# Context keys in a strand of their own, even groups' heads copied in place, normalising on ScalarE

## The reference, cut to what matters

```python
x = _layernorm(x + gated_linear_recurrence(x))
x = _layernorm(x + window_attention(x, ctx, ctx))        # WINDOW: 4 windows of 128
x = _layernorm(x + quantised_lora_ffn(x))                # 256 -> 1024 -> 256, GELU
x = _layernorm(x + alibi_attention(x, x, x))             # ALIBI
x = _layernorm(x + masked_attention(x, ctx, ctx, group)) # MASKED: probs * group
x = _layernorm(x + latent_attention_and_moe(x))          # CAUSAL, then top 2 of 8 experts
# attention: softmax(q @ k.T / 4 (+ bias, + mask)) @ v, heads joined, @ w_out
```

## Time and profile before

| | us |
|---|---|
| median of 3 runs | 1575.84 (1571.24 to 1581.65) |
| the profiled execution | 1581.31 |
| its span, first to last instruction | 1579.3 |
| TensorE busy | 1432.0 (91%) |
| VectorE busy | 1098.5 (70%) |
| ScalarE busy | 757.2 (48%) |
| GpSimd busy | 137.6 (9%) |
| chain that ended last | PE 71%, DVE 9%, issue 7%, SPq 6%, ACT 3% |

### The profile page before, as it was taken

One profiled execution on the slowest core, in us unless ns is written; L12 is line 12 of the kernel. 1 busy time (PEld: TensorE's weight loads), 2 busy tenths in 40 slices (PEclk: granted clock), 3 DMA queues, 4 the chain that ended last, 5 costly groups with the idle time before them and its releaser, 6 DMA issues.

```text
span 1579.3 us, 29394 instructions
## 1 busy us (share of the span) xinstructions
PE 1432.0 (91%) x9731; PEld 805.2 (51%) x9764; DVE 1098.5 (70%) x2504; ACT 757.2 (48%) x1434; POOL 137.6 (9%) x126
## 2 busy tenths in 40 slices
PE   7788889999999999999999999999999959887990
PEld 3566565653654535343343343434455526777990
DVE  4897855673664667799999999997878845331523
ACT  4454644348346474645455444545565534322330
POOL 1001101100100100000000000000000030021304
PEclk7899999999999999999999999999999969998996
DMA  6332342302303221233222232021321252864862
GB/s 201 95 104 58 113 113 64 112 8 76 99 2 92 85 82 49 53 92 101 61 87 62 75 120 51 2 52 46 80 73 50 53 171 73 300 234 161 263 201 87
DMA packets 119345, 154.06 MB, mean 98 GB/s; under 512 B 31746, under 2 KB 99714, under 8 KB 117250
## 3 DMA queue, kind: packets, MB, share of 16 engines
q1 hardware_dynamic: 116132, 143.80, 30.7%
q0 software_dynamic: 3072, 8.39, 1.7%
HBM read 73.23 MB, written 18.35 MB: 58 GB/s over the span
## 4 chain that ended last, share of the span: by engine, by line
PE 71%; DVE 9%; issue 7%; SPq 6%; ACT 3%; DMA 2%; POOL 1%; DVEq 0%; POOLq 0%; ACTq 0%
PE ps L1132 24%; PE ps L1323 9%; PE ps L1360 6%; PE ps L1288 4%; SPq L1038 3%; PE ps L1283 3%; PE ps L1280 3%; PE ps L1351 3%; PE ps L1226 3%; PE ps L1355 2%; PE ps L1322 2%; PE ps L1290 2%; PE ps L1330 2%; DVE ps L1824 2%; ACT prob L1543 2%
## 5 line engine op out<-in xcount | busy, mean ns | idle before, releaser
L1543 ACT ACTIVATE prob<-ps 128x512 f32<-128x512 f32 (+3 forms) x832 | 407.3, 548 | 239.1 <-PE ps L1323 117.5
L1828 DVE TENSOR_REDUCE mx<-ps 128x1 f32<-128x512 f32 (+3 forms) x512 | 278.8, 584 | 108.4 <-PE ps L1290 51.4
L1323 PE MATMUL ps<-of_expert 99*128 99x512 bf16 (+4 forms) x768 | 253.3, 357 | 11.1 <-ACT prob L1543 4.5
L2000 DVE SCALAR_TENSOR_TENSOR room_b<-room_b,ps 128x512 f32<-128x512 f32 x46 | 31.6, 687 | 135.1 <-ACT room_b L1578 122.1
L1323 PEld LDWEIGHTS ps<-of_expert 99*128 99x128 bf16 (+1 forms) x768 | 73.4, 98 | 95.5 <-ACT prob L1543 42.3
L1610 POOL TENSOR_TENSOR rstd<-ve,half 128x4 f32<-128x4 f32 x28 | 31.3, 1118 | 1033.2 <-DVE ve L1757 744.6
L1360 PE MATMUL ps<-prob,va 128*32 128x512 f32 (+3 forms) x1024 | 115.7, 524 | 0.2
L1283 PE MATMUL ps<-of_expert 96*128 96x512 bf16 x256 | 89.4, 380 | 11.6 <-DVE mx L1824 9.5
L1288 PE MATMUL ps<-of_expert 102*128 102x512 bf16 x256 | 93.6, 382 | 1.5 <-issue 1.0
L1280 PE MATMUL ps<-of_expert 96*128 96x128 bf16 (+3 forms) x256 | 72.4, 307 | 18.4 <-issue 9.5
L1824 DVE CUSTOM_DVE_ANT_0 ps<-ps,room_a 128x512 f32<-128x512 f32 x128 | 85.7, 708 | 3.9 <-PE ps L1283 3.4
(11 more groups left out here) (216 smaller groups left out, 2556.8 us busy)
## 6 DMA issues: line engine op xcount, KB each, us to landing
of_expert<-parts SPq DMA_DIRECT2D x384, 128.0 KB, 2.4
room_a<-in_w SPq DMA_DIRECT2D x38, 512.0 KB
room_b<-in_w SPq DMA_DIRECT2D x18, 512.0 KB
otc<-oraw SPq DMA_DIRECT2D x256, 32.0 KB, 2.0
sorted<-y SPq DMA_DIRECT2D x2, 2944.0 KB, 10.8
pack<-sorted SPq DMA_DIRECT2D x46, 128.0 KB
expert_out<-room_b SPq DMA_DIRECT2D x46, 128.0 KB
ct<-in_c SPq DMA_DIRECT2D x8, 512.0 KB, 4.3
```

The source lines that it names most:

```text
L1323: i = pe.matmul(dst[:, lo:S], ks[0:rows, h, t], qs[0:rows, h, lo:S], start=(a != MASKED), stop=(a != CAUSAL and not fixed))
L1543: act.activation(prob[:, quad % PROBS, n, lo:S], key_bank(*st)[:, lo:S], ACT.Exp).then_inc(s_exp, 1)
L1828: i = dve.tensor_reduce(mx[:, slot, s, n:n + 1], src[:, 0:width], AX.X, ALU.max)
```

## The change

What it does, edit by edit:

- Keys and values from the context (units of WINDOW and MASKED) get a strand of their own, `context`. Only the queries stay behind `TR`. The key product no longer waits for `xt` nor for the scaled query weights. `SL` is split by operand instead of by half (`SL, u, o`), `rest` is doubled, and the operand DMAs of queries and keys have semaphores of their own.
- `C` of an even group: ScalarE copies the bank straight into `otc`, which is now double, one for each of two units in turn; heads lie 32 rows apart. `C` of an odd group: as before to `oraw`, and four DMAs set its heads in the gaps, after the even group's sums have landed. The rows of the output weights are put in that sequence on the host (`by_turns`). The sums' DMA also waits for the reciprocals' DMA of the pair before.
- `LZ` runs on ScalarE: four activations `Identity` with scale and bias of 128x256. For it GpSimd makes `shift`, minus mean times the power, in two more instructions of 128x4 after the power.
- `va` holds a head in 17 columns instead of 32; a weight load still takes 32, with the next head's values in the upper rows of the product.
- The planner's costs are a little different (SyncE 0.6 for 0.5 a DMA, others), and every number of `LAG` is new, so `ORDER` is another list.

```diff
-FAMILY = {"RS": "LS", "RZ": "LZ", "FS": "LS", "FZ": "LZ"}
+FAMILY = {"RS": "LS", "FS": "LS", "FZ": "RZ"}
...
-    return {0: 0, 2: 0, 5: 0}.get(n, 1)
+    return {0: 3, 2: 0, 5: 0}.get(n, 1)
...
-        for c in range(NC):
-            before += [("QK", u, 0, c), ("QK", u, 1, c), ("SL", u, c)]
-        before += [("VP", u, 0), ("VP", u, 1)]
+        strand = context if a in (WINDOW, MASKED) else before
+        strand += [("QK", u, 1, 0), ("QK", u, 1, 1), ("SL", u, 1)]
+        if strand is before:
+            before += [("QK", u, 0, 0), ("QK", u, 0, 1), ("SL", u, 0)]
+        strand += [("VP", u, 0), ("VP", u, 1)]
+        if strand is context:
+            before += [("QK", u, 0, 0), ("QK", u, 0, 1), ("SL", u, 0)]
...
-    return [first, kept, added, normed, ops, turned, values, recips, normal, loads, outs, mask, weights, rows, before, later, routes, sums, grouped,
+    return [first, kept, added, normed, ops, turned, values, recips, normal, loads, outs, mask, weights, rows, context, before, later, routes, sums, grouped,
...
-        return [("DVE", 2.5, [src]), ("POOL", 1.0, [])]
+        return [("DVE", 2.5, [src]), ("POOL", 1.9, [])]
...
-        return [("DVE", 1.7, [(("LS", b, n), "POOL")])]
+        return [("ACT", 1.6, [(("LS", b, n), "POOL")])]
...
-LAG = {"IN": -1.4, "EA": -1.5, "CA": -9.3, ("CA", 0): 9.5, ("CA", 1): 9.4, "FS": -7.3, "FZ": -1.0, "SO": -6.2, "OP":
...
+LAG = {"EA": -1.0, ("CA", 0): -6.9, ("CA", 1): 11.9, "FS": -12.1, "FZ": 11.0, "SO": 8.6, "OP": -12.7, ("OP", 0):
...
-        va = [sb(f"va{i}", [P, NT, H, 32]) for i in range(2)]
+
+        va = [sb(f"va{i}", [P, NT, H * (HD + 1) + 32 - HD - 1]) for i in range(2)]
         ones = sb("ones", [P, 32])
         prob = sb("prob", [P, PROBS, J, S])
-        rest = sb("rest", [P, NC, S])
+        rest = sb("rest", [P, 2, NC, S])
         parts = sb("parts", [P, 2, 3, NC, S], BF16)
-        oraw = [sb(f"oraw{i}", [P, S]) for i in range(2)]
-        otc = sb("otc", [P, NC, S])
+        oraw = sb("oraw", [P, S])
+        otc = [sb(f"otc{i}", [P, NC, S]) for i in range(2)]
...
-            return s_op[mine], 16 * 2 * len(Q_PARTS) * sum(mine in pieces(v) for v in range(u + 1))
+            return s_op[o][mine], 16 * len(Q_PARTS) * sum(mine in pieces(v) for v in range(u + 1))
...
-                    sp.wait_ge(s_p2, nth("SL", u, g // 2))
+                    sp.wait_ge(s_p2, nth("SL", u, o))
...
-                    i = g % 2
+                    i, pair = g % 2, 2 * u + g // 2
+                    into = otc[u % 2][:, g // 2, :]
                     sp.wait_ge(s_oc, nth("C", u, g))
-                    sp.dma_start(sums[i][:, :], oraw[i][HD:P:32, :]).then_inc(s_spread[i], 16)
-                    if u:
-                        sp.wait_ge(s_ou, nth("OU", u - 1, 1))
-                    for n in range(J):
-                        at = 64 * i + HD * n
-                        sp.dma_start(otc[at:at + HD, g // 2, :], oraw[i][32 * n:32 * n + HD, :]).then_inc(s_packed[i], 16)
+                    if pair:
+                        sp.wait_ge(s_rows[i], 16 * pair)
+                    sp.dma_start(sums[i][:, :], (oraw[HD:P:32, :] if i else into[HD:P:32, :])).then_inc(s_spread[i], 16)
+                    if i:
+                        sp.wait_ge(s_spread[0], 16 * (pair + 1))
+                        for n in range(J):
+                            sp.dma_start(into[32 * n + HD:32 * n + 2 * HD, :], oraw[32 * n:32 * n + HD, :]).then_inc(s_packed, 16)
                 elif kind == "R":
                     u, g = st[1:]
                     i = g % 2
@@ -1074,7 +1097,7 @@
                     before = 2 * u + g // 2 - 1
                     if before >= 0:
                         sp.wait_ge(s_o, nth("N", before // 2, before % 2))
...
-                    pe.wait_ge(s_ws, nth("WS", a))
                     pe.wait_ge(s_wa, 16 * (a + 1))
-                    pe.wait_ge(s_xt, nth("TR", u, 1, 1))
+                    pe.wait_ge(s_pack, 16)
+                    if not o:
+                        pe.wait_ge(s_ws, nth("WS", a))
+                    if not o or a in (ALIBI, CAUSAL):
+                        pe.wait_ge(s_xt, nth("TR", u, 1, 1))
...
+                elif kind == "LZ":
+                    b, n = st[1:]
+                    i_ = norm_buffer(n)
+                    act.wait_ge(s_rstd, nth("LS", b, n))
+                    for t in range(NT):
+                        i = act.activation(x[b][:, t, :], x[b][:, t, :], ACT.Identity, bias=shift[:, i_, t:t + 1], scale=rstd[:, i_, t:t + 1])
+                    i.then_inc(s_lnorm, 1)
...
-                    u, c = st[1:]
-                    act.wait_ge(s_f, nth("QK", u, 1, c))
-                    act.activation(parts[:, :, 1, c, :], rest[:, :, :], ACT.Copy).then_inc(s_p1, 1)
+                    u, o = st[1:]
+                    act.wait_ge(s_f, nth("QK", u, o, 1))
+                    act.activation(parts[:, o, 1, :, :], rest[:, o, :, :], ACT.Copy).then_inc(s_p1, 1)
...
-                    i_ = g % 2
-                    before = 2 * u + g // 2
+                    pair = 2 * u + g // 2
                     act.wait_ge(s_pv, nth("V", u, g, quads(u) - 1))
-                    if before:
-                        act.wait_ge(s_spread[i_], 16 * before)
-                        act.wait_ge(s_packed[i_], 16 * J * before)
-                    act.activation(oraw[i_][:, :], bank(V_BANK), ACT.Copy).then_inc(s_oc, 1)
+                    if g % 2 == 0:
+                        if u > 1:
+                            act.wait_ge(s_ou, nth("OU", u - 2, 1))
+                        act.activation(otc[u % 2][:, g // 2, :], bank(V_BANK), ACT.Copy).then_inc(s_oc, 1)
+                    else:
+                        if pair:
+                            act.wait_ge(s_spread[1], 16 * pair)
+                            act.wait_ge(s_packed, 16 * J * pair)
+                        act.activation(oraw[:, :], bank(V_BANK), ACT.Copy).then_inc(s_oc, 1)
                 elif kind == "HT":
...
-                    pool.tensor_tensor(rstd[:, i_, :], ve[:, i_, :], half[:, :], ALU.pow).then_inc(s_rstd, 1)
+                    if kind == "RS":
+                        pool.tensor_tensor(rstd[:, i_, :], ve[:, i_, :], half[:, :], ALU.pow).then_inc(s_rstd, 1)
+                    else:
+                        pool.tensor_tensor(rstd[:, i_, :], ve[:, i_, :], half[:, :], ALU.pow).then_inc(s_g, mine.one())
+                        pool.wait_ge(s_g, mine.count)
+                        pool.tensor_tensor(shift[:, i_, :], mv[:, i_, :, 0], rstd[:, i_, :], ALU.mult).then_inc(s_g, mine.one())
+                        pool.wait_ge(s_g, mine.count)
+                        pool.tensor_scalar(shift[:, i_, :], shift[:, i_, :], -1.0, None, ALU.mult).then_inc(s_rstd, 1)
...
+                    before = norm_before(st)
+                    if before and before[0] == "LS":
+                        dve.wait_ge(s_lnorm, nth("LZ", *before[1:]))
...
-                elif kind == "LZ":
-                    b, n = st[1:]
-                    i_ = norm_buffer(n)
-                    dve.wait_ge(s_rstd, nth("LS", b, n))
-                    for t in range(NT):
-                        i = dve.tensor_scalar(x[b][:, t, :], x[b][:, t, :], mv[:, i_, t, 0:1], rstd[:, i_, t:t + 1], ALU.subtract, ALU.mult)
-                    i.then_inc(s_norm, 1)
...
-                        dve.wait_ge(s_packed[i_], 16 * J * (2 * u + c + 1))
+                    dve.wait_ge(s_oc, nth("C", u, 2 * c))
+                    dve.wait_ge(s_packed, 16 * J * (2 * u + c + 1))
+                    heads = otc[u % 2][:, c, :]
                     dve.stream_shuffle(rinv[:, :], rs[:, :], [0] * HD + [HD] * HD).then_inc(s_v, mine.one())
                     dve.wait_ge(s_v, mine.count)
-                    dve.tensor_tensor(otc[:, c, :], otc[:, c, :], rinv[:, :], ALU.mult).then_inc(s_o, 1)
+                    dve.tensor_tensor(heads, heads, rinv[:, :], ALU.mult).then_inc(s_o, 1)
                 elif kind == "OU":
...
+def by_turns(np, m):
+
+    return np.ascontiguousarray(m.reshape(NC, 2, J, HD, D).transpose(0, 2, 1, 3, 4)).reshape(m.shape)
```

More of the change, by code:

```diff
@@ L880, in decoder @@
         s_alibi = [sem(f"alibi_of_quarter_{g}_loaded") for g in range(G)]
-        s_op = [sem(f"operands_of_quarter_{g}_loaded") for g in range(G)]
+        s_op = [[sem(f"{name}_of_quarter_{g}_loaded") for g in range(G)] for name in ("queries", "keys")]
         s_ml = [[sem(f"mask_{i}_of_{b}_loaded") for i in range(3)] for b in range(2)]
@@ L893, in decoder @@
         s_spread = [sem(f"sums_{i}_spread") for i in range(2)]
-        s_packed = [sem(f"heads_{i}_packed") for i in range(2)]
+        s_packed = sem("odd_heads_packed")
         s_rows = [sem(f"reciprocals_{i}_in_rows") for i in range(2)]
@@ L1270, in _ @@
                     rows = ALL_ROWS - 3 if a == ALIBI else ROWS
-                    pe.wait_ge(*op_ready(u, g))
+                    for o in range(2):
+                        pe.wait_ge(*op_ready(u, g, o))
```

119 lines of the change are left out of this document (68 added, 51 removed), and 27 rows, old and new, of the table LAG.

## The result

The changed kernel takes 1586.08 us (median of 9 runs, 1582.68 to 1589.7), the kernel before 1578.31 beside it (9 runs): a ratio of 1.0051, 95% interval 1.0034 to 1.0068. The forecast was 1553 with a range of 1528 to 1578. It is outside the range and, by a little, on the other side: 8 us slower, clear of the noise of these runs.

What follows compares the result with a forecast made beforehand. It took TensorE (320 to 657, 1048 to 1240 us), VectorE in masked attention and, in places before 320, SyncE's DMA issuing as limits. Terms summed to -23.1 us from the 1575.84 median: 1553, range 1528 to 1578.

Steps and rivals of the forecast that it cites:

- What bounds the kernel: Masked attention, 657 to 1048 us: VectorE, busy 372.5 of 391 us, was taken as nearer the limit than TensorE.
- Start, -4.7: Kernel start: context keys and values computed before normalising ends bring the first score to 50.7 us for 55.4, -4.7 us.
- Later window units, -7: Three more window units: context keys and values leave the path between x and the scores, -7 us, bounds 0 and -21.
- Even groups, -6.0 and -1: 128 of 256 head DMAs go: -6.0 us before 320 us, -1 us from 1240 to 1320.
- Normalising, -5.4, -2 and +3: Moved to ScalarE: VectorE relief -5.4 us in masked stretch, -2 before 320; exponentials delayed in ScalarE's queue, +3.
- ScalarE becomes late: Rival: in TensorE-bound stretches normalising delays exponentials, +33 for +3, up to 1590; chance 0.13 together with a worse order.
- The port lock: Rival: 40 added GpSimd steps block VectorE, +6.2 us masked, +4.5 in first stretch, 1563; chance 0.27 with two others.
- Planning anew, 0 (+13, -12): Whole kernel: the newly planned order of steps, priced by no row, taken as 0, between +13 and -12 us.

Runs made afterwards that it cites:

- g1: e2 with only the first of four tiles normalised in each layer norm, the rest left as they are: ratio 0.9990 to the kernel before.
- i1: The kernel before, unchanged, run again for a second trace: ratio 1.0003.
- f0: The changed kernel itself, run again as the level for others in its batch: ratio 1.0071 to the kernel before.
- f3: The changed kernel with only the first of four tiles normalised in each layer norm: ratio 1.0052 to the kernel before.
- h2: The changed kernel planned anew with other numbers in LAG, nothing else: ratio 1.0066 to the kernel before.
- h4: The changed kernel with the context strand in window units only, not masked ones, and LAG sought anew: ratio 1.0029 to the kernel before.
- e3: The kernel before, its order untouched, with only the even groups copied in place and odd groups by transfer: 1539.9 us, ratio 0.9953.
- i2: e3 run again in a later batch: ratio 0.9950 to the kernel before.
- f2: The changed kernel with normalising back on VectorE, placed 7 steps behind its statistics: ratio 1.0238 to the kernel before.
- e2: The kernel before, its order untouched, with normalising on ScalarE and two extra GpSimd steps: 1568.28 us, ratio 1.0140.
- g2: e2 with the shift left out, so the mean isn't subtracted: ratio 1.0047 to the kernel before.

## Why the prediction was wrong, by its own steps

The sum was -23.1 us and the measured change is +8. Two steps failed most: the order, put at 0, and the normalising, put at -5.4 and -2.

**What bounds the kernel.** From 657 to 1048 us VectorE's share was read rightly, but what it is spared there can hardly be cashed in. TensorE's matmuls wait for it only 11.8 us in all in that stretch, and 11.2 after the change. In g1, which spares VectorE all its normalising and gives ScalarE a quarter of it, first masked to first causal score takes 389.8 us for 390.7 (i1) and 391.1 (before).

**Start, -4.7: right in size.** First score at 49.2 for 55.4 (or 52.6, i1); the five traces with the strand and ScalarE's normalising in an order planned for both (after, f0, f3, h2, h4) have 47.1 to 50.2, the thirteen of before and of kernels built on it 51.7 to 56.9. Inside it, two terms were off against each other: GpSimd's two steps took 0.43 us of work and not 2.0, ScalarE's normalising 2.06 and not 1.6. Part of the gain has another source: the power itself ended at 25.4 and not at 30.5, as the new order starts the first block sooner.

**Later window units, -7: not found.** The scores of the window units end at 259.8 for 256.1, after starting 6 us earlier. SyncE did leave the chain, and TensorE's projections took its place (L1155 28.4% for L1132's 22.7% in the earlier trace rows).

**Even groups, -6.0 and -1: right** in the order of before, with -6.7 by the length of the window stretch and -7.3 (e3) and -8 (i2) in all.

**Normalising, -5.4, -2 and +3: a step that failed.** It has three faults. The price: 0.41 us from a square without pointers per partition, where this form takes 0.587, so the block, whose four instructions overlap a little, is 2.08 us and not 1.65. The relief: g1 gains about 1 us in the masked stretch and 1.5 in all (0.9990, 0.9973 to 1.0006), and in f2 the reverse move costs 1.8 there, so -5.4 was several times too large. And the queue: 0 to 33 us was right as a range, but +3 was chosen from loads that wait for exponentials. That row hardly moves (42.3, 44.9 after), while in the order of before the matmuls' own waits for exponentials rise two and a half to three times and the move costs 20 to 22 us net. The rival "ScalarE becomes late" had this mechanism; e2's ratio of 1.014 is beyond that rival's 1590 (1.009), but only in an order not made for the edit. In the changed kernel itself +3 stands (f3).

**The port lock.** VectorE's total fell by 24.4 us, where its 80 normalisings had taken 32.6. The GpSimd steps that the change adds did VectorE little harm: in e2, which has all 40, its total fell by 30.4. They were themselves held up in a few places, up to 1202 ns for a median of 228 beside a VectorE step. What hurt was the old bias addition at a new place: of 15 small steps L1888 in the masked stretch one took 1970 ns and of 15 of L1882 one 1701, each beside that addition, the others 175. That is the exclusion which the Trainium skill (SBUF — State Buffer, the reading of its port diagram) describes, and the traces agree with it. It isn't the rival's +6.2 from 40 added steps; it is 3.3 us of VectorE, of which TensorE waited for one, and a lower clock behind it. And the four normalisings of e3 above, 3.05 us beside a GpSimd addition, show that the old place paid too, where hardly anything waited.

**Planning anew, 0 (+13, -12): the step that failed most.** No row priced it, and the middle of its bounds was taken. The order of before was a good one for its work: both other orders of it cost 7.4 and 8.4 us, and a new order for e3 cost 14.6, more than the upper bound. With the start at -4.7, the even groups at -7.3, the later units at 0 and the normalising at about -2 and +3, the sum would be -11. The 19 us from there to +8 are left for the order and the strand together, an estimate by difference. Set against e3, the only part with a gain by itself, the changed kernel is 16 us slower (1.0051 against 0.9953 and 0.9950); f3 bounds ScalarE's work in it at about 3 of these, h4 returns 6.5 with the masked strand off and a new order. What in the order costs the time is shown at one place only, the masked stretch with its held-up step and lower clock. How the rest divides between the strand, the extra filler and the order stays open. It can't be told by edits in one order, because the parts don't add up across orders: the same engine move costs 20 to 22 us in one and saves 26 to 37 in the other.

## What to carry to other kernels

Where one list of steps fixes the queues of all engines, an edit is two changes: the work and the order. Time the part alone in the old order before planning anew, and time a new order with no work changed; here the first gave the only gain (e3), and the second costs as much as most edits bring. A step on the path from one block to the next needs its price as the delay until its result is ready and its engine free, and everything that the engine copies for the bounding one stands behind it. Read a wait where it ends last: a load that waits for an exponential may cost nothing, a matmul that does stops TensorE. And count the records, but put a missing matmul back at the pace of its neighbours, not at its full duration: 33 missing ones of 379 ns hid about 2 us.

## What the runs showed of the hardware

- ScalarE on 128x256, f32 to f32, takes 587 ns with a scale and a bias per partition (L1515), 498 with the scale alone and a constant bias (g2), against 414 for a square with its sum, which writes bf16. VectorE's two-pointer form takes 406 as a median.
```profile
L1494 ACT ACTIVATE x<-x,rstd x80: 491/498/528, 29.9 to 1115.8; 128x256 f32<-128x256 f32 x80
```
- GpSimd on 128x4: a power 1.04 us, a product 0.20, a product with a constant 0.23. At one size the operation makes a difference of five times.
- A VectorE step of 128x16 with two SBUF inputs, 174 ns otherwise, took 1970 ns when it began 60 ns behind a GpSimd addition of 128x1024; TensorE then stood still for 2.26 us, and its granted clock was 0.50 in 671.4 to 674.8 us.
- The same kernel differs by 2% between batches of runs, and not evenly. e3 and i2 are one kernel: the expert stage took 193 us from its first turning to its last in e3 and 214 in i2, the causal scores 258 and 272, while the stages before agree within 1%.
